# Batch-norm statistics read straight from PSUM, a bias as a product row, and last sums as products with ones, in a recommender kernel

## What is computed

```python
B, F_CAT, F_CONT, V, D = (2048, 26, 13, 12500, 64)
H1, H2 = (1024, 512)
def _batchnorm(x, g, b):
    mu = jnp.mean(x, axis=0)
    var = jnp.mean((x - mu) ** 2, axis=0)
    return g * (x - mu) * jax.lax.rsqrt(var + BN_EPS) + b
...
first_cat = cat_t1[fidx, cat_feats]
fm_first = jnp.sum(first_cat, axis=1) + jnp.sum(first_cont, axis=1)
emb_cat = cat_t2[fidx, cat_feats]
emb_cont = cont_t2[None, :, :] * cont_feats[:, :, None]
E = jnp.concatenate([emb_cat, emb_cont], axis=1)
s = jnp.sum(E, axis=1)
fm_second = 0.5 * jnp.sum(s * s - jnp.sum(E * E, axis=1), axis=1)
deep = E.reshape(E.shape[0], -1)
h = jax.nn.relu(_batchnorm(deep @ W1 + b1, g1, be1))
h = jax.nn.relu(_batchnorm(h @ W2 + b2, g2, be2))
deep_out = (h @ W3 + b3)[:, 0]
out_pos = jax.nn.sigmoid(bias + fm_first + fm_second + deep_out)[:, None]
return jnp.concatenate([1.0 - out_pos, out_pos], axis=1)
```

## Time and profile before

| | us |
|---|---|
| median of 3 runs | 871.62 |
| lowest and highest run | 866.34, 873.04 |
| profiled execution: span from first to last instruction | 645.4 |
| what the median has beyond that span | 226.2 |
| PE busy / ACT busy / DVE busy / POOL busy | 522.1 / 191.7 / 216.2 / 399.0 |
| last gather issued | 529.4 |
| PE's first product of layer 2 | 541.25 |
| PE's last product of layer 2 | 630.75 |

### The profile page before, as it was taken

How to read it: one execution, slowest core, us unless ns; L and a number is a source line. 1 busy time by engine, 2 the same in 40 slices (tenths; PEclk the granted TensorE clock), 3 DMA queues, 4 the chain that set the end, 5 groups by cost and what they waited for, 6 DMA issues and landing times.

```text
span 645.4 us, 9108 instructions
## 1 busy us (share of the span) xinstructions
PE 522.1 (81%) x3324; PEld 467.0 (72%) x3324; DVE 216.2 (33%) x428; ACT 191.7 (30%) x405; POOL 399.0 (62%) x423
## 2 busy tenths in 40 slices
PE   0839999969766977698679966997698778999993
PEld 0139989968766877687577956796688777788882
DVE  1362252214221422142205220522052235654366
ACT  1351231212111211121113110321031225897655
POOL 5787777777777777777777777777777760000000
PEclk9958997997999798979987999788979878999996
DMA  8963234323332333234323432333234520000000
GB/s 284 296 133 28 29 28 28 27 26 27 27 28 25 28 27 26 27 28 27 27 27 26 27 28 27 26 28 26 27 27 60 123 25 0 2 1 1 1 0 1
DMA packets 18021, 26.74 MB, mean 41 GB/s; under 512 B 7602, under 2 KB 7834, under 8 KB 18010
## 3 DMA queue, kind: packets, MB, share of 16 engines
q0 software_dynamic: 13312, 13.87, 27.5%
q1 hardware_dynamic: 4384, 12.66, 5.5%
q10 hardware_dynamic: 314, 0.07, 0.1%
HBM read 26.56 MB, written 0.02 MB: 41 GB/s over the span
## 4 chain that ended last, share of the span: by engine, by line
POOL 54%; issue 19%; PE 16%; DMA 4%; DVE 3%; ACT 3%; POOLq 0%; SPq 0%; DVEq 0%; ACTq 0%
POOL emb L249 54%; PE bank L696 10%; DMA h<-in_w 4%; PE bank L631 2%; PE bank L658 2%; ACT h L388 1%; PE bank L681 1%; DMA emb<-in_table,idx_now 1%; DVE h L612 0%; DVE stats L557 0%; ACT hhi L351 0%; PE bank L731 0%; DVE stats L490 0%; DVE mv L544 0%; DVE zpart L592 0%
## 5 line engine op out<-in xcount | busy, mean ns | idle before, releaser
L249 POOL DMA_INDIRECT emb<-in_table,idx_now x416 | 398.2, 957 | 130.7 <-issue 130.7
L658 PE MATMUL bank<-xhi,w1hi 128*128 128x256 f32 x832 | 254.6, 306 | 0.0
L658 PE MATMUL bank<-xlo,w1hi 128*128 128x256 f32 x832 | 245.4, 295 | 0.0
L658 PE MATMUL bank<-xhi,w1lo 128*128 128x256 f32 x832 | 244.9, 294 | 0.0
L658 PEld LDWEIGHTS bank<-xhi,w1hi 128*128 128x128 f32 x832 | 170.0, 204 | 0.0
L658 PEld LDWEIGHTS bank<-xlo,w1hi 128*128 128x128 f32 x832 | 170.0, 204 | 0.0
L658 PEld LDWEIGHTS bank<-xhi,w1lo 128*128 128x128 f32 x832 | 169.1, 203 | 0.0
L442 DVE TENSOR_TENSOR xlo<-bank,xhi 128x256 fp32r<-128x256 f32 x104 | 44.0, 423 | 351.6 <-ACT xhi L282 351.6
L282 ACT ACTIVATE xhi<-bank 128x256 fp32r<-128x256 f32 x104 | 39.8, 383 | 377.4 <-PE bank L646 377.4
L646 PE MATMUL bank<-ident,emb 128*128 128x128 f32 x208 | 45.6, 303 | 76.7 <-DMA emb<-in_table,idx_now 74.8
L646 PEld LDWEIGHTS bank<-ident,emb 128*128 128x128 f32 x208 | 23.7, 146 | 93.0 <-DMA emb<-in_table,idx_now 85.3
(11 more groups left out here) (68 smaller groups left out, 288.1 us busy)
## 6 DMA issues: line engine op xcount, KB each, us to landing
h<-in_w SPq DMA_DIRECT2D x13, 512.0 KB, 16.0
emb<-in_table,idx_now POOLq DMA_INDIRECT x416, 3.3
h<-in_w SPq DMA_DIRECT2D x1, 3072.0 KB, 12.6
w2raw<-in_w SPq DMA_DIRECT2D x8, 256.0 KB, 5.5
h<-in_w SPq DMA_DIRECT2D x1, 256.0 KB, 13.4
idx_all<-in_cat SPq DMA_DIRECT2D x1, 208.0 KB, 2.8
cont_sb<-in_cont_t SPq DMA_DIRECT2D x8, 13.0 KB
diag<-in_cont_diag ACTq DMA_DIRECT2D x1, 45.5 KB, 3.0
```

What stands on the lines that cost most here:

```text
L249: nc.gpsimd.indirect_dma_start(out=emb[:, j, at:at + ROW], out_offset=None, in_=table, in_offset=bass.IndirectOffsetOnAxis(ap=idx_now[:, j ...
L658: done = nc.tensor.matmul(acc[c], w[:, k, cols], x[:, s, :], start=False, stop=(last and n == 2), skip_group_check=True)
```

## The change

Five edits go together. (1) The last block's first-layer sums are no longer evicted before their statistics: `last_stats` reads `acc[c]` in the bank, and ACT evicts later, between the first hidden tiles. (2) The first batch norm has five parts, (0), (1), (2, 3), (4, 5), (6, 7), interleaved by hand with statistics, `hlo` and evictions; ACT's `hidden` is split into `hidden_high` and `hidden_full`. (3) b1 is a 14th row of `m_sb`, multiplied by a row of ones in `cont_sb`, so statistics from a bank contain it. In layer 2 `statistics2` also reads the bank, b2 is added to the mean instead (an operation with three operands), and ACT evicts only after the statistic. (4) PE's last block is written out behind a loop of seven: the product of pair k-1 stands before the transpose of pair k, and `multiply_last` takes the products with `xhi` of a bank's two feature groups first. (5) In the tail, the last m's first tile is normalised and weighted by DVE, its last tile is read by ACT from the bank with a shift `out_shift` that holds b2, and the four transposes and reductions per quarter become products of `u`'s tiles with a column of ones, 20 in all, added up in one bank; `zsum` reads that bank.

```diff
-NORM_PARTS = [(0, 2), (2, C1)]
+NORM_PARTS = [(0, 1), (1, 2), (2, 4), (4, 6), (6, 8)]
...
+            sp.wait_ge(cont_ones, 1)
             with sp.Fori(0, BLOCKS) as b:
...
+            act.dma_start(m_sb[CONT:CROWS, :], b1_row).then_inc(b1_in, 16)
...
+            nc.vector.memset(cont_sb[:, :], 1.0).then_inc(cont_ones, 1)
...
+            def last_sums_out(m):
+                act.wait_ge(stats1_done, C1 * (BLOCKS - 1) + 2 * m + 2)
+                sums_out(BLOCKS - 1, m)
...
             def sums2_out(n, m):
-                act.wait_ge(acc2_full, n * C2 + m + 1)
+                act.wait_ge(stats2_done, n * C2 + m + 1)
...
+            def last_stats(c):
+                dve.wait_ge(acc_full, b * ACC_BANKS + (c // 2 + 1 + EMPTY))
+                nc.vector.bn_stats(stats1[:, c, b, :], acc[c]).then_inc(stats1_done, 1)
...
             def statistics2(n, m):
-                dve.wait_ge(acc2_free, n * C2 + m + 1)
-                nc.vector.bn_stats(stats2[:, m, n, :],
-                                   h1[:, m, n * NB2:(n + 1) * NB2]).then_inc(stats2_done, 1)
+                dve.wait_ge(acc2_full, n * C2 + m + 1)
+                nc.vector.bn_stats(stats2[:, m, n, :], bank2(n, m)).then_inc(stats2_done, 1)
...
+            nc.vector.scalar_tensor_tensor(out=out_shift[:, :], in0=scale, scalar=b2[:, m:m + 1], in1=shift,
+                                           op0=ALU.mult, op1=ALU.add).then_inc(shift_ready, 1)
+            own = h1[:, m, 0:NB2]
+            nc.vector.tensor_scalar(own, own, scale, shift, ALU.mult, ALU.add).then_inc(own_step, 1)
+            dve.wait_ge(own_step, 1)
+            nc.vector.tensor_scalar(own, own, 0.0, w3[:, m:m + 1], ALU.max, ALU.mult).then_inc(own_step, 1)
+            for n in range(1, N2):
+                dve.wait_ge(out2_ready, m * N2 + n)
+                weighted(m, n)
...
+            def multiply_last(b):
+                k = KT - 1
+                pe.wait_ge(xhi_ready, KT * (b + 1))
+                pe.wait_ge(w1_ready, k + 1)
+                for m in range(ACC_BANKS):
+                    pair = (2 * m, 2 * m + 1)
+                    for c in pair:
+                        product(k, c, w1hi, xhi)
+                        product(k, c, w1lo, xhi)
+                    if m == 0:
+                        pe.wait_ge(split_done[k % TP], TP_USES[k % TP] * b + (k // TP + 1 + EMPTY))
+                    for c in pair:
+                        done = product(k, c, w1hi, xlo, stop=True)
+                    done.then_inc(acc_full, 1)
...
+            for k in range(1, KT):
+                multiply(b, k - 1)
+                transpose(b, k)
+            multiply_last(b)
...
+            def z_part(x, t, w, start, stop):
+                return nc.tensor.matmul(z[:, t:t + 1], x[:, t * P:(t + 1) * P], w, start=start, stop=stop,
+                                        skip_group_check=True)
```

More of the change, by code:

```diff
@@ L42, with build @@
 EMPTY = 1
-NORM_PARTS = [(0, 2), (2, C1)]
+NORM_PARTS = [(0, 1), (1, 2), (2, 4), (4, 6), (6, 8)]
 FM_STEPS = 8
-PAR = 3 * C1 + 4 * C2 + 2
-def build(nc, table, cat, cont_t, cont_tab, cont_diag, w1, w2, params, out):
+PAR = 2 * C1 + 4 * C2 + 2
+CROWS = CONT + 1
+def build(nc, table, cat, cont_t, cont_tab, cont_diag, w1, w2, b1_row, params, out):
     f32, f32r = mybir.dt.float32, mybir.dt.float32r
@@ L122, in build @@
     prob = place("prob", [P, TILES, 2], f32)
-    zpart = place("zpart", [P, TILES], f32)
+    ones = place("ones", [P, 1], f32)
+    out_shift = place("out_shift", [P, 1], f32)
     W2RAW_KT, W2LO_KT = 3, 7
@@ L367, in _ @@
             act.wait_ge(norm1_ready, 1)
-            for k in range(early):
-                hidden(0, k)
-            sums_out(b, 2)
-            sums_out(b, 3)
-            std(bn1, mv1, *NORM_PARTS[1], mean1_ready, std1_ready)
-            act.wait_ge(norm1_ready, 2)
-            for k in range(early, C1):
-                hidden(0, k)
+            hidden_high(0, 0)
+            std1(1)
+            hidden_full(0, 0)
+            act.wait_ge(norm1_ready, 2)
+            hidden_high(0, 1)
+            hidden_full(0, 1)
@@ new lines, in _ @@
+            std1(2)
+            last_sums_out(0)
+            act.wait_ge(norm1_ready, 3)
+            hidden_high(0, 2)
+            hidden_full(0, 2)
+            last_sums_out(1)
+            std1(3)
+            hidden_high(0, 3)
+            hidden_full(0, 3)
+            act.wait_ge(norm1_ready, 4)
+            hidden_high(0, 4)
+            hidden_full(0, 4)
+            std1(4)
+            last_sums_out(2)
+            hidden_high(0, 5)
+            hidden_full(0, 5)
+            last_sums_out(3)
@@ L376, in _ @@
+            act.wait_ge(norm1_ready, 5)
+            for k in range(6, C1):
+                hidden_high(0, k)
+                hidden_full(0, k)
             square(b, len(GROUPS) - 1)
@@ new lines, in _, with transpose @@
+            pe.wait_ge(b1_in, 16)
+            def transpose(b, k):
+                s = k % TP
+                pe.wait_ge(gathered[k], 16 * 2 * BT * (b + 1))
+                pe.wait_ge(split_done[s], TP_USES[s] * b + (k // TP + EMPTY))
+                for j in range(BT):
+                    done = nc.tensor.transpose(tp[s][:, j * P:(j + 1) * P],
+                                               emb[:, j, k * PAIR + 1:k * PAIR + 1 + P], ident[:, :])
+                done.then_inc(transposed, 1)
@@ new lines, in product, with multiply @@
+            def product(k, c, w, x, stop=False):
+                return nc.tensor.matmul(acc[c], w[:, k, c * P:(c + 1) * P], x[:, k % XT, :], start=False,
+                                        stop=stop, skip_group_check=True)
+            def multiply(b, k):
+                pe.wait_ge(split_done[k % TP], TP_USES[k % TP] * b + (k // TP + 1 + EMPTY))
+                pe.wait_ge(w1_ready, k + 1)
+                last = k == KT - 1
+                for c in range(C1):
+                    product(k, c, w1hi, xhi)
+                    product(k, c, w1hi, xlo)
+                    done = product(k, c, w1lo, xhi, stop=last)
+                    if last and c % 2:
+                        done.then_inc(acc_full, 1)
+                if not last:
+                    done.then_inc(x_used[k % XT], 1)
```

237 lines of the change are left out of this document (134 added, 103 removed).

## The result

| | before | after |
|---|---|---|
| median of 4 runs, us | 870.33 | 880.02 |
| lowest and highest run | 866.34, 873.04 | 879.30, 882.78 |
| ratio to before, 95% interval | | 1.0109 (1.0073 to 1.0145) |
| span of the profiled execution | 645.4 | 877.8 |
| time of that execution | not given | 879.54 |

The account below looks back on a forecast made before the run. Gathers were taken to bound the kernel up to the last one, then a chain of waits; 3.4 + 2.05 + 0.7 + 3.25 = 9.4 us off gave span 636.0, with 226.2 around it 862.2 us, range 857.5 to 867.0.

Parts of the forecast that it names:

- a gather queue: Up to the last gather: POOL's gathers set the pace, other engines' work costs nothing within 65 us a block.
- that I leave as it is: Around the profiled span: 226.2 us of the 871.62 median, kept unchanged in the forecast.
- Last block on PE: Block 7, product k-1 before transpose k: last transpose about 0.4 us late, first bank full 1.9 us earlier.
- First normalisation: Between layers 1 and 2: PE starts layer 2 3.4 us earlier, including 1.9 from the last block.
- First tiles and the eviction: Layer 2: first two tiles lose 0.45 instead of 2.5, gaining 2.05 us; last quarter's eviction before statistics goes, 0.7 us.
- Tail: From the last statistics to `zsum`: four reductions and the exchange with PE disappear, 3.25 us gained.
- Own tile: Tail, DVE's tile of the last row group: two operations at 0.49 us, 1.0; bound 0.75 each.
- Statistics from a bank: Statistics reading PSUM: no surcharge given, against 0.065 us more per statistic by the Trainium skill's page.
- Straight-line code feeds PE slowly: Rival, block 7 written out: products at 0.2277 us, 17.7 us later, minus 9.4, so 880; chance 0.03.
- A cover breaks: Rival, layer 2's second quarter: FM sums or evictions keep PE waiting, half of 5.45 us lost, 865 to 867; chance 0.10.
- little ahead of the tail: Rival, before the tail: PE not really held by the first normalisation, 3.95 us gained, 867.7; chance 0.04.
- The clock takes back the start of layer 2: Rival, start of layer 2: half-speed stretches lose 1.7 or 3.4 us, 864 to 865.6; chance 0.18.

Follow-up runs that it names:

- e4: Changed kernel with PE's layer 1 as one loop of eight, old order in the last block too, no `multiply_last`; quiet chip: 645.35 us, 0.9952 of before.
- e3: Changed kernel with PE's first seven blocks written out too, on a quiet chip: 642.80 us, 0.9917 of before.
- e8: Changed kernel plus 16 unread products that keep PE busy ahead of the last products with ones, quiet chip: 642.43 us, 0.9899 of before.
- e1: Kernel before, unchanged, profiled again on a quiet chip: 648.89 us, 1.0008 of before.
- e5: Changed kernel, unchanged, run again on a quiet chip: 643.33 us, 0.9907 of before.
- e17: Changed kernel with transposes ahead of products up to pair 11, changed order for the last pair only; stalling chip: 867.11 us, 0.9978 of before.
- e2: Kernel before with PE's loop over eight blocks written out, on a quiet chip: 647.94 us, 0.9996 of before.
- e14: Kernel before with all eight of PE's blocks written out, on another visit to a quiet chip: 649.65 us, 1.0002 of before.
- e16: Kernel before with all eight of PE's blocks written out, on a stalling chip: 867.49 us, 0.9988 of before.
- hybrid order: Changed kernel with the old order, transposes ahead of products, up to pair 11 and the new order for the last pair alone: 0.9978 stalling, 0.9922 quiet.
- e15: Changed kernel with transposes ahead of products up to pair 11, changed order for the last pair only; quiet chip: 644.37 us, 0.9922 of before.
- e12: Changed kernel with hybrid order and 16 unread products that keep PE busy before the end, stalling chip: 875.34 us, 0.9902 of before.
- e9: Kernel before with PE's block 7 behind 330 unread products that make PE late, stalling chip: 954.70 us, 1.0785 of before.

## Why the prediction was wrong

**The step that failed** is its first: "So up to the last gather the kernel is a gather queue, and what other engines do in the first seven blocks costs nothing while it fits into 65 us a block". In the runs that were to be predicted it did not fit: a block took 90 to 102 us. With it went "that I leave as it is" about the 226.2 us around the span. A third of the median was not in the profile, and I took it for a constant of the launch. It was a second condition of the same program, with another bound: PE, held at "issue", with some 45 us of work left at the last gather. The difference could have been read as a warning that the trace at hand was not of the runs to be predicted. From the trace of before alone its nature could not be known, but the rival "PE is late" could have been asked: with PE behind, what does each edit cost? The order of block 7 would have answered: ACT's copy and DVE's difference at each pair, against the 1.9 us that I counted as its gain. That is the term that turned the sign.

**Last block on PE.** In the quiet condition the step holds. From the landing of the last gather to layer 2's first product it takes 7.00 us in e4, with the old order (532.22 to 539.22), and 5.24 and 4.89 in e3 and e8: 1.8 and 2.1 gained, forecast 1.9. I priced only the last transpose ("about 0.4 us late") because I took PE for waiting on gathers. Where PE is late, the eleven gaps cost 13.2 us, and the 12.5 above is what is left with all gains up to layer 2 taken off.

**First normalisation**, forecast 3.4, the 1.9 included: 8.42 before (534.13 to 542.55 in e1) less 5.24 and 4.89 is 3.2 and 3.5; counted from the last gather's issue, e1 against e5, it is 3.35. e3's 5.24 us (forecast 5) begin where the last gather landed, at 534.92. Its rows:

```profile
535.86 0.42 DVE L490 TENSOR_TENSOR xlo<-bank,xhi 128x256 fp32r<-128x256 f32 x1 [3.88 <-ACT xhi L288]
...
536.89 0.43 DVE L596 BATCH_NORM_STATS2 stats<-bank 128x6 f32<-128x256 f32 x1 [0.61 <-PE bank L736]
...
538.94 0.81 ACT L362 ACTIVATE hhi<-h,bn 128x512 fp32r<-128x512 f32 x1 [0.88 <-DVE bn L590]
```

**First tiles and the eviction**, forecast 2.05 + 0.7 = 2.75: from layer 2's first product to the last statistics e1 took 542.55 to 634.28, 91.73 us, e5 539.77 to 628.54, 88.77. That is 2.96. The chain of e5 has layer 2 unbroken, so neither the clock nor a cover took anything back there, nor in e17 (71.31 us for the same 312 products on a stalling chip):

```profile
539.77 71.32 PE bank L813 x312
```

**Tail**, forecast 3.25: from the last statistics to `zsum` 9.87 us before (634.28 to 644.15 in e1, and the same in the earlier trace rows), 10.54 in e5 and 10.13 in e3. So 0.3 to 0.7 lost, where 3.25 was to be gained. The mis-sized term is "loading the same tile stays, 128 columns become one, so 1.0": I counted the last four products only, as one pass each. All 16 wait together, for DVE's own tile first, and take 32 passes at 0.22 us (7.00/32) on a PE that had gone down to half clock. At full clock they are not free either: e8's 3.73 us for the 32 leave 2.6 of the 3.25. Own tile (0.54 + 0.48), `out_shift` (0.22) and the three weighted sums (2.07) were as forecast.

**Statistics from a bank** took 0.686 us on the mean in e5 for 512 elements, like those from SBUF (0.682), and 0.406 for 256, where they took 0.417 from SBUF before. An estimate by the Trainium skill ("VectorE: DVE Perf Modes", the TRN2 errata) would have had 0.065 us more each; by these runs the surcharge is not there.

**Sum.** For the quiet condition, 3.35 + 2.96 - 0.67 = 5.6 against 9.4, and less 0.57 for a gather queue that ended later it is the 5.0 between the spans of e1 and e5; the medians gave 5.6 (e3) and 6.7 (e5). What is missing from 9.4 is the tail (3.25 forecast, 0.67 lost). For the stalling condition, in which the forecast was to be met, 12.2 lost up to layer 2 and 2.3 gained behind it, 9.9 slower.

**The rivals.** None was right. "Straight-line code feeds PE slowly" comes out at 880, the very number measured, and by the wrong road: written-out code ran at the loop's pace in e2, e14 and e16 (0.9996, 1.0002, 0.9988). A rival that hits the number is not thereby confirmed. "A cover breaks" is refuted by the unbroken chain, "little ahead of the tail" by the 3.35 and 2.96. "The clock takes back the start of layer 2" happened in one trace, small: in e3 PE stood 1.64 us before the last transpose, the granted clock was 0.50 from 537.20 to 540.10, its last 24 products of layer 1 took 4.49 us, and layer 2 began at 540.16, 0.4 later than in e5; 0.2 of it was left at the last statistics (628.72 against 628.54). In e5 the clock was 1.00 there. The clock's larger part was at the tail, where I had not looked.

**Versions that beat before in both conditions.** The hybrid order does: e17 0.9978 stalling (0.9958 to 0.9998, so barely), e15 0.9922 quiet. It isn't free on a quiet chip: with pairs 10 and 11 both ahead of the last transpose, e15 takes 10.6 us from the last gather to layer 2 (531.45 to 542.08), where e5 takes 9.1 and the old order 10.5 (e4). With PE kept busy ahead of the last products e12 has 0.9902 on a stalling chip. That is 6.6 us better than e17 on another stalling chip, and the tail explains 3 of them; the rest is not explained. On a quiet chip the warm tail ran only with the changed order (e8, 0.9899).

**What stays open.** Why a chip is in the one condition or the other; and whether it is the gathers that hold PE, and by what. The profile says "issue" and no more. In these traces the stalls occur only with gathers in flight; gathers alone are not enough, as the quiet chips have the same gathers at 957 and 960 ns (before, e5). No experiment here changed the number or the size of the gathers.

## What to carry to other kernels

Compare the profile's span with the runs' times before reading anything in it: 226 us of 872 between them meant that the profile was of another condition with another bound, and the first step worked out from it, the gather queue, did not hold in the runs. When the order of a pipeline is changed to gain at its last element, price all the elements for the case that their engine is the late one: an element that waits for its own split costs ACT's and DVE's time at each, eleven times 1.20 us here, for a gain of 1.9 where the gathers are late. And an engine that idles before a short burst at the end may do that burst at half clock: count all of its instructions, its passes, and the rate of a cold engine.

## What the runs showed of the hardware that I had not expected

On two chips of five, and on that of the result, PE waits on "issue" while indirect gathers are in flight: single f32r products 0.7 to 2 us apart instead of 0.119, 26 to 36 us per block of 90 to 102 in the result's profile, 153 to 183 us over the pairs' products (result, e16, e9), with a program that takes 648 to 650 us elsewhere and 868 or 885 there. Looped and written-out code are hit alike (152.7 and 161.5 us). It lets the sign of one change depend on the condition: 1.0114 and 1.0109 there, 0.9907 on a quiet chip.

An f32 product with a column of ones (128x128 times 128x1) is recorded as two passes, 0.44 us together at a granted clock of 0.50 (7.00/16) and 0.23 in e8 (3.73/16).

A standstill of PE of 3.9 us ahead of the products with ones was followed by a granted clock of 0.50 in e5, with 1.00 in the 80 us before it. In e8, where 16 large products lay in that standstill, the clock stayed at 1.00 over the products with ones; the mean of 0.80 in the longer stretch includes the time behind them. The rows are e8's:

```profile
545.00:625.00 80.00, 80.00 (x354) 66.26 (x354) 45.40 (x94) 61.60 (x97) 0.00 (x0) 1.00 0.00 1
...
632.00:635.90 3.90, 3.81 (x33) 3.65 (x32) 2.11 (x4) 2.59 (x4) 0.00 (x0) 1.00 0.00 0
632.00:639.00 7.00, 3.82 (x33) 3.65 (x32) 2.46 (x6) 2.81 (x5) 0.00 (x0) 0.80 0.02 2
```
